# Two experts picked in slot 31 from 14 batches' first choices, and a drain in another order

## The reference

```
logits = x @ gate_w.T
probs = jax.nn.softmax(logits, axis=-1)
top2_w, top2_idx = jax.lax.top_k(probs, 2)
cap = int(CAPACITY_FACTOR * T / E)            # 640 of 4096 tokens
counts = jnp.bincount(top2_idx.reshape(-1), length=E)
keep = (counts <= cap).astype(x.dtype)
comb = jnp.zeros((T, E)).at[jnp.arange(T)[:, None], top2_idx].add(top2_w) * keep[None, :]
h = jax.nn.relu(jnp.einsum('th,ehf->tef', x, W1) + b1)
y = jnp.einsum('teh,ehf->tef', h, W2) + b2
out = jnp.einsum('te,tef->tf', comb, y)
```

## Time and profile before

| | |
|---|---|
| median of three runs | 516.7 us (516.62 to 518.55) |
| profiled execution | 519.01 us, span 517.0 us |
| granted PE clock, mean | 0.993 |
| busy: PE, DVE, ACT, POOL | 499.2, 401.2, 371.2, 324.0 us |

### The profile page before, as it was taken

The page is one execution under the profiler, slowest core; times in us unless marked ns, Lnnn a source line. Parts: engine busy times, 40 slices in busy tenths (PEclk is TensorE's granted clock), DMA queues, the critical chain, the costliest instruction groups (busy, mean ns, idle before and its releaser), DMA issues.

```text
span 517.0 us, 12870 instructions
## 1 busy us (share of the span) xinstructions
PE 499.2 (97%) x3896; PEld 348.6 (67%) x3896; DVE 401.2 (78%) x715; ACT 371.2 (72%) x851; POOL 324.0 (63%) x328
## 2 busy tenths in 40 slices
PE   7899999999999999999999999999999989889997
PEld 6866667666666777766676667666666756666664
DVE  4234788888888888888888888888888797736766
ACT  3467777777777777777777777777777437657873
POOL 1102677777777777777777777777777549004760
PEclk9999999999999999999999999999999989999999
DMA  6500000000000000000000000000000000000004
GB/s 221 155 1 2 2 1 2 1 0 0 0 0 0 0 0 0 0 0 0 0 0 0 0 0 0 0 0 0 0 0 2 1 1 0 2 0 2 0 21 143
DMA packets 9364, 7.19 MB, mean 14 GB/s; under 512 B 1088, under 2 KB 8832, under 8 KB 9216
## 3 DMA queue, kind: packets, MB, share of 16 engines
q1 hardware_dynamic: 9344, 6.94, 4.6%
HBM read 4.84 MB, written 2.10 MB: 13 GB/s over the span
## 4 chain that ended last, share of the span: by engine, by line
PE 89%; DVE 5%; issue 2%; ACT 2%; DMA 1%; SPq 1%; POOL 1%; DVEq 0%; ACTq 0%; POOLq 0%
PE bank_a L704 11%; PE misc L711 11%; PE bank_d L719 11%; PE bank_t L686 11%; PE bank_s L671 7%; PE bank_d L696 6%; PE bank_t L953 4%; PE bank_t L681 4%; PE misc L841 3%; PE misc L843 3%; PE misc L808 2%; PE bank_s L961 2%; PE bank_d L961 2%; PE misc L868 1%; PE bank_a L642 1%
## 5 line engine op out<-in xcount | busy, mean ns | idle before, releaser
L1374 POOL TENSOR_TENSOR pair<-kx 128x1152 f32<-128x1152 f32 x32 | 82.9, 2591 | 96.6 <-DVE shifted L422 77.7
L300 DVE TENSOR_REDUCE row_max<-bank_s 128x4 bf16<-128x512 f32 x128 | 89.4, 699 | 67.7 <-PE bank_s L671 67.7
L1339 POOL TENSOR_TENSOR mix_hi<-mix_hi 128x512 f32<-128x512 f32 (+2 forms) x96 | 79.7, 831 | 3.1
L1007 ACT ACTIVATE qT<-misc 128x512 f32<-128x512 f32 x64 | 39.1, 611 | 53.7 <-PE misc L711 53.6
L1007 ACT ACTIVATE prob<-bank_t 128x512 f32<-128x512 f32 x128 | 69.7, 603 | 4.4 <-PE bank_t L686 2.8
L719 PE MATMUL bank_d<-attT,wpost_sb 128*128 128x128 f32 x512 | 69.2, 278 | 0.2 <-DVE attT L308 0.2
L711 PE MATMUL misc<-yT,wq_sb 128*128 128x128 f32 x512 | 67.7, 275 | 0.0
L704 PE MATMUL bank_a<-prob,v 128*32 128x512 f32 x512 | 67.4, 598 | 0.0
L686 PE MATMUL bank_t<-qT,kT 64*128 64x256 f32 x512 | 65.7, 376 | 0.0
L1345 POOL TENSOR_TENSOR mix_hi<-weight,kx 128x1024 f32<-128x1024 f32 x32 | 63.1, 1973 | 0.3 <-ACT weight L1007 0.3
L711 PEld LDWEIGHTS misc<-yT,wq_sb 128*128 128x128 f32 x512 | 62.2, 192 | 0.8
(11 more groups left out here) (183 smaller groups left out, 934.9 us busy)
## 6 DMA issues: line engine op xcount, KB each, us to landing
out<-acc_all SPq DMA_DIRECT2D x8, 256.0 KB, 2.3
x_all<-in_xT SPq DMA_DIRECT2D x1, 1024.0 KB, 9.7
w_sb<-in_w SPq DMA_DIRECT2D x2, 512.0 KB
x_all<-in_xT SPq DMA_DIRECT2D x1, 768.0 KB, 7.6
wq_sb<-in_wq SPq DMA_DIRECT2D x1, 512.0 KB, 6.2
wpost_sb<-in_wpost SPq DMA_DIRECT2D x1, 512.0 KB, 9.8
x_all<-in_xT SPq DMA_DIRECT2D x1, 256.0 KB, 3.2
b_rows<-in_b SPq DMA_DIRECT2D x16, 4.0 KB
```

The source lines that it names most:

```text
L300: V.tensor_reduce(bass.AP(row_max, first_w * (P + 1) + HPG * p, [[HPG * P, P], [P + 1, 2], [KEY, 2], [1, 1]]), bank_s[:, :, :].rearrange(" ...
L1007: return nc.scalar.activation(out_, in_, func, **kw)
L1339: G.tensor_tensor(mix_hi[:, jd, 0:r, :], mix_hi[:, jd, 0:r, :], mix_hi[:, jd, r:2 * r, :], ALU.add).then_inc(s_hi, 1)
L1374: G.tensor_tensor(pair[:, :, :], bass.AP(kx2, jc * 2 * P, [[4 * P, P], [0, SHIFTS], [1, P]]), bass.AP(kx2, jc * 2 * P, [[4 * P, P], [MD, S ...
```

## The change

1. First choices of 14 batches (COUNTED) instead of 24 make the pick. Logits of batches 0 to 5 and 6 to 13 stay in slot 31, the first group no longer ahead of the last scores; those of 14 to 23 come in the drain, behind unit 0. ACT copies the EARLY logits there, too.
2. `pick_ahead` stands at the end of slot 31, right behind the second `normalise`, instead of in slot 32 behind `weight_sums` and `weight_inverses`. Its intermediate values lie in PSUM (bank_s); the key formula is done twice, once into PSUM and once into SBUF.
3. In slot 32 `weighted_rows` comes before the head copies, `weight_sums` and `weight_inverses` behind the shift. `keys_twice` waits for the first quarter of `s_lo` and `s_hi` (the products that read the keys) only.
4. The count product stands behind units 12 and 13 instead of ahead of them. Only one group of x1 transposes (into misc[1]) comes before the loop's first hidden products, seven behind them; the banks of bank_x are in another order.

```diff
@@ -33,6 +33,7 @@
+COUNTED = range(14)
@@ -157,14 +158,15 @@
-        bank_x = [b[:, :].rearrange("p (t f) -> p t f", f=P) for b in bank_a] + [misc[1][:, :, :]]
+        wide_a = [b[:, :].rearrange("p (t f) -> p t f", f=P) for b in bank_a]
+        bank_x = [misc[1][:, :, :]] + wide_a
         bank_e = [bank_s, bank_d]
-        bank_b = bank_x[0:2] + [misc[0][:, :, :], misc[1][:, :, :]]
+        bank_b = wide_a + [misc[0][:, :, :], misc[1][:, :, :]]
         def key_out(b):
-            return misc[1][:, 0:1, :] if s_is(b, BATCH - 1) else bank_x[1][:, 0:1, :]
+            return misc[1][:, 0:1, :] if s_is(b, BATCH - 1) else wide_a[1][:, 0:1, :]
@@ -354,23 +356,23 @@
-            def ranked(into):
-                step(V.tensor_tensor(t88[:, :, :], key[:, :].unsqueeze(1).to_broadcast(wide),
-                                     key[:, :].unsqueeze(2).to_broadcast(wide), ALU.is_lt))
-                step(V.tensor_reduce(place[:, :], t88[:, :, :], AX.X, ALU.add))
-                step(V.tensor_tensor(t88[:, :, :], index8[:, :].unsqueeze(2).to_broadcast(wide),
-                                     place[:, :].unsqueeze(1).to_broadcast(wide), ALU.is_equal))
-                step(V.tensor_tensor(t88[:, :, :], t88[:, :, :], index8[:, :].unsqueeze(1).to_broadcast(wide), ALU.mult))
-                step(V.tensor_reduce(order_f[:, :], t88[:, :, :], AX.X, ALU.add))
+            def ranked(into, key, same, place, t88):
+                step(V.tensor_tensor(t88, key.unsqueeze(1).to_broadcast(wide),
+                                     same.unsqueeze(2).to_broadcast(wide), ALU.is_lt))
+                step(V.tensor_reduce(place, t88, AX.X, ALU.add))
+                step(V.tensor_tensor(t88, index8[:, :].unsqueeze(2).to_broadcast(wide),
+                                     place.unsqueeze(1).to_broadcast(wide), ALU.is_equal))
+                step(V.tensor_tensor(t88, t88, index8[:, :].unsqueeze(1).to_broadcast(wide), ALU.mult))
+                step(V.tensor_reduce(order_f[:, :], t88, AX.X, ALU.add))
...
-                dve.wait_ge(s_log_mm, 4)
+                dve.wait_ge(s_log_mm, 2)
                 dve.wait_ge(s_const, 3)
-                top, fi = part(r_max, EARLY), part(first, EARLY)
-                lg = misc[0][:, :, :].rearrange("p w f -> p (w f)")[:, 0:len(EARLY) * EXPERTS].rearrange(
+                top, fi = part(r_max, COUNTED), part(first, COUNTED)
+                lg = misc[0][:, :, :].rearrange("p w f -> p (w f)")[:, 0:len(COUNTED) * EXPERTS].rearrange(
@@ -379,10 +381,13 @@
-                step(V.scalar_tensor_tensor(out=key[:, :], in0=bank_s[:, 0, 0:EXPERTS], scalar=float(EXPERTS),
-                                            in1=index8[:, :], op0=ALU.mult, op1=ALU.add))
-                ROUTE_STEPS["pick"] = ranked(ahead_order)
-                step(V.tensor_scalar(not_ahead[:, :], place[:, :], float(AHEAD), None, ALU.is_ge))
+                rank, spot = bank_s[:, 1, 0:EXPERTS], bank_s[:, 1, EXPERTS:2 * EXPERTS]
+                for t in (rank, key[:, :]):
+                    step(V.scalar_tensor_tensor(out=t, in0=bank_s[:, 0, 0:EXPERTS], scalar=float(EXPERTS),
+                                                in1=index8[:, :], op0=ALU.mult, op1=ALU.add))
+                ROUTE_STEPS["pick"] = ranked(ahead_order, rank, key[:, :], spot, bank_s[:, 2, 0:EXPERTS * EXPERTS].rearrange(
+                    "p (a b) -> p a b", b=EXPERTS))
+                step(V.tensor_scalar(not_ahead[:, :], spot, float(AHEAD), None, ALU.is_ge))
@@ -498,23 +503,22 @@
                         normalise(s, 0)
                     if s_is(s, BATCH - 1):
                         normalise(s, 1)
+                        pick_ahead()
                 def drain_slot():
-                    if s == BATCH:
-                        weight_sums()
-                        weight_inverses()
-                        pick_ahead()
                     if C:
                         attended()
                     head_scores()
+                    if s == BATCH:
+                        weighted_rows()
                     own_copies()
                     head_maxima()
                     head_shift()
                     if D:
+                        weight_sums()
+                        weight_inverses()
                         if s > BATCH:
-                            weight_sums()
-                            weight_inverses()
-                        weighted_rows()
+                            weighted_rows()
                         row_sum()
                         rows_joined()
                         mixed()
@@ -721,7 +725,7 @@
-            parts_early = [EARLY[a:b] for a, b in ((0, 6), (6, 13), (13, 19), (19, 24))]
+            parts_early = [EARLY[a:b] for a, b in ((0, 6), (6, 14), (14, 24))]
@@ -730,19 +734,23 @@
+                if tiles == parts_early[2]:
+                    pe.wait_ge(s_rt, ROUTE_STEPS["tops"])
...
-                              tok_all[:, col(b)], gate_sb[:, :], start=(b in (EARLY[0], RECENT[0])), stop=True,
+                              tok_all[:, col(b)], gate_sb[:, :], start=(b in (EARLY[0], parts_early[2][0], RECENT[0])), stop=True,
...
-                pe.wait_ge(s_ao, UNITS)
+                pe.wait_ge(s_kx2, BATCH)
                 for q in quads:
+                    if 0 < q < len(bank_x):
+                        pe.wait_ge(s_ao, UNITS - len(bank_x) + 1 + q)
@@ -810,8 +818,6 @@
-                    if final:
-                        gate_logits(parts_early[0])
@@ -843,7 +849,7 @@
-                        gate_logits(parts_early[1])
+                        gate_logits(parts_early[0])
@@ -859,8 +865,7 @@
-                        gate_logits(parts_early[2])
-                        gate_logits(parts_early[3])
+                        gate_logits(parts_early[1])
@@ -906,7 +911,9 @@
                         ahead_hidden(1)
                         keys_turned(c)
                         pe.wait_ge(s_x1T, n(c))
-                        ahead(0, 1, 2)
+                        ahead(0)
+                        gate_logits(parts_early[2])
+                        ahead(1, 2)
                         mixing_turned(d)
                         ahead(3)
                         tokens_made(d)
@@ -933,11 +940,12 @@
             slots(pe, slot)
+            ahead(12, 13)
             pe.wait_ge(s_log, 2)
             pe.wait_ge(s_rt, ROUTE_STEPS["count"])
             mm(misc[0][:, 0, 0:EXPERTS], ones[:, :], count[:, :], start=True, stop=True).then_inc(s_cnt_mm, 1)
-            ahead(12, 13, 14, 15)
-            x1_transpose(range(HALF))
+            ahead(14, 15)
+            x1_transpose(range(1))
             def bias_rows(quads):
@@ -970,7 +978,7 @@
-            x1_transpose(range(HALF, QUADS))
+            x1_transpose(range(1, QUADS))
@@ -1048,8 +1056,6 @@
-                if tiles[0] in EARLY:
-                    act.wait_ge(s_rt, ROUTE_STEPS["tops"])
@@ -1120,8 +1126,8 @@
-                    need(act, s_lo, 4 * n(c - 2))
-                    need(act, s_hi, 4 * n(c - 2))
+                    need(act, s_lo, 4 * (c - 2) + 1)
+                    need(act, s_hi, 4 * (c - 2) + 1)
@@ -1140,7 +1146,6 @@
-                        copy_logits(EARLY, 4)
@@ -1151,7 +1156,9 @@
                         ahead_relu(1)
                         keys_twice()
                         head_weights()
-                        ahead(0, 1, 2)
+                        ahead(0)
+                        copy_logits(EARLY, 3)
+                        ahead(1, 2)
                         mixing_out(d)
                         ahead(3)
                         tokens_out(d)
@@ -1168,7 +1175,7 @@
-                        copy_logits(RECENT, 6)
+                        copy_logits(RECENT, 5)
@@ -1255,9 +1261,10 @@
             set_expert(0, e)
             runs = act.value_load(n_run[0:1, 0:1], min_val=3, max_val=EXPERTS - 1)
             act.wait_ge(s_b1, 1)
+            copy_x1(range(1))
             for i in range(2):
                 relu(i + 1, i)
-            copy_x1(range(HALF, QUADS))
+            copy_x1(range(1, QUADS))
             act.wait_ge(s_rt, ROUTE_STEPS["loop"])
             set_gate(0, e)
             act.wait_ge(s_gT_mm, 1)
```

More of the change, by code:

```diff
@@ L545, in _ @@
                                         op0=ALU.mult, op1=ALU.add))
-            ROUTE_STEPS["order"] = ranked(order)
+            ROUTE_STEPS["order"] = ranked(order, key[:, :], key[:, :], place[:, :], t88[:, :, :])
             step(V.tensor_reduce(kept[:, :], keep_loop[:, :], AX.X, ALU.add))
@@ L1230, in _ @@
             ahead(12, 13, 14, 15)
-            copy_x1(range(HALF))
             def set_gate(k, e):
```

## The result

In the first comparison (four executions of each kernel in turn on one chip) the changed kernel took 511.6 us in the median (510.87 to 511.86), the kernel before 516.66 us: ratio 0.989, 95% interval 0.987 to 0.992, faster by 5.1 us. The forecast was 510.3 with a range of 508.0 to 513.6.

What follows compares the result with a forecast made beforehand. PE, busy 499.2 of 517.0 us, was the bound. Loop start 8.1 us sooner less 1.64 for extra copies gave 6.4 us (pick 4.0, count 2.4); from the 516.7 us median this made 510.3, range 508.0 to 513.6.

Steps and rivals of the forecast that it cites:

- Slot 31: Logits of ten batches move from slot 31 behind the drain's first unit, so batch 31's normalisation comes 2.27 us sooner.
- The pick: Choosing the first expert on VectorE from PSUM takes 1.8 us instead of 3.2, or 3.4 if GpSimd still slows it.
- First product: PE's first expert product at 417.4 us instead of 421.07, after a stop of 1.1 us, with full clock behind it.
- Unit 1: The drain's unit 1 starts at 423.8 us where it was 426.60, 2.8 us ahead.
- Mixing: Drain: batch 30's mixing follows the pair product 7.7 us later, at 431.5, before PE's 434.8; the 1.22 us stop goes.
- Count: Final count: its 2.24 us stop goes; the loop's first hidden product comes 8.1 us sooner, behind a 2.1 us stop.
- Copies: Loop's first hidden product to gate transposes: seven residual copies instead of four, paced by ScalarE, 6.44 us instead of 4.80.
- Rival 1: Behind the first expert's stop: the clock gain is absent or the low clock stays, 1.4 us less, 511.7 us; chance 0.17.
- 1.42 us regained: First product to first output group: 2.35 us at full clock instead of 3.77 at half clock.
- Rival 2: The remaining 2.1 us stop ahead of the loop lowers the clock, 1.8 us more, 512.1 us; chance 0.08.
- rival 3: Drain: mixing still sets PE's place, the sooner pick buys nothing, only the count's 2.4 us, 514.3 us; chance 0.09.
- Rival 4: Fourteen batches pick an expert the count throws out; the loop runs four experts, 14.9 us more, 525.2 us; chance 0.03.

Runs made afterwards that it cites:

- e4: Changed kernel with the pick's intermediate values back in SBUF and one key formula, at the new place: 512.53 us, ratio 0.991 to the kernel before.
- e7: Changed kernel with the pick's last reduction written to PSUM and the cast reading it there: 510.33 us, ratio 0.986 to the kernel before.
- e8: Changed kernel with the order and waits of the mixing (part 3) as before: 512.53 us, ratio 0.992 to the kernel before.
- e11: e10 with residual copies of groups 2, 4 and 6 moved from ScalarE to VectorE: 510.04 us, ratio 0.985 to the kernel before.
- The parts alone: Kernel before with only parts 1 to 3 (e3, again e12): 514.13 and 514.57 us; with only part 4 (e2): 515.48 us.
- e9: Changed kernel again, no edit: 511.14 us against 518.14 for the kernel before, ratio 0.986.
- e5: Kernel before with 16 dummy products instead of 6 ahead of the pick: 517.79 us, ratio 1.000 to the kernel before.
- e6: Changed kernel without the six dummy products ahead of the pick: 512.50 us, ratio 0.991 to the kernel before.
- e12: Same kernel as e3, run once more: 514.57 us, ratio 0.994 to the kernel before.
- e3: Changed kernel with part 4 undone, so only parts 1 to 3 (pick and mixing): 514.13 us, ratio 0.992 to the kernel before.
- e10: e7 with ScalarE loading the loop's first expert once the order is there, ahead of the number of passes: 509.76 us, ratio 0.985 to the kernel before.
- e2: Kernel before with only part 4 (later count product, one x1 group ahead of the loop): 515.48 us, ratio 0.996 to the kernel before.
- e1: Kernel before again, no edit: 517.39 us, ratio 0.999 to the kernel before.

## Why the prediction was right, step by step

Gains here are before less after, each from its first score product (0.91 us off each difference of starts).

- **Slot 31.** 2.27 us predicted; the second normalisation ended at 412.36 instead of 415.52, 2.25.
- **The pick.** The lower bound of 1.8 us was taken for it; it took 412.28 to 414.88, 2.60. PSUM cost next to nothing (0.23 us a step with 64 values, 0.22 from SBUF in the earlier trace rows), and e4 shows that SBUF would have cost 2.25. The missing term is the cast, the one instruction left with only SBUF operands. I had priced it like its neighbours, at 0.26 with the gap. By the prediction's argument, that an instruction with a single SBUF input is not held up, it was free; the 0.88 us here and the 0.17 of e7 show that for the cast this is false.
- **First product.** 417.4 was predicted, 416.71 measured, of which 0.9 is the shorter start-up: 3.45 us sooner, not 3.67. The stop was 1.34 us (1.1 predicted). The clock stayed at 1.00. From the first product to the first output group it took 2.54 us; 2.35 predicted, 3.77 before.
- **Unit 1.** 2.44 us sooner, not 2.8: about the two misses above, 0.22 and 0.19 us.
- **Mixing.** No stop, as predicted, but with no slack: ready at 434.05 and turned by PE at 434.20, where the forecast had 431.5 (430.6 with the shorter start-up) and 3.3 us of slack. The pair product was on time (419.97). Two terms failed here. The first is "DVE's rest of that slot, about 5 us": batch 29's mix rows, two SBUF operands, took 1.88 us beside POOL's product instead of the 0.29 that the row of before at 426.46 has. By starting POOL sooner part 3 put its product beside them; in e8, without part 3, they took 0.29 again. The second is "follows 7.7 us later": no row gives this number. From DVE's first score step of that slot to the end of batch 30's mix rows it was 9.46 us in the kernel before (429.21 to 438.67) and 9.46 in the changed one (424.59 to 434.05). In the changed one the mix rows took 2.09 us, but they had taken 1.25 before as well, so this part was a misjudged size and no effect of the change. The mixing came 3.5 us later than forecast against 3.3 us of forecast slack, and PE, itself 0.3 us later than forecast, just did not have to stop: that was luck. The 1.22 us of the earlier trace rows came back all the same; e8 shows that without part 3 they would not have. PE began the hidden product of unit 13 (449.57 before, 444.95 now) 3.71 us sooner (4.0 predicted).
- **Count.** No stop there, as predicted; the loop's first hidden product 8.25 us sooner (8.1), behind a stop of 1.54 us (2.1).
- **Copies.** 6.27 us for 6.44. Gates 6.78 us sooner (6.4 predicted). The reason given, that ScalarE paces them, does not hold alone: e11 takes three of the seven copies off ScalarE, and the transposes end no sooner (5.38 us against 5.36).

The sum of 6.4 us stood against 6.6 to 6.9 by the body. The parts alone were predicted at 4.0 and 2.4 and measured at 3.7 and 2.75. That the time came out at 511.6 and not 510.3 is not a failed step. The forecast subtracted it from 516.7, the median of three runs; in later comparisons the kernel before had medians of 517.3 to 518.1 over 11 to 27 executions. That the start-up's scatter made this difference is likely, not shown; it moves the first score product by up to 4 us between profiles. The interval of the first comparison (4.3 to 6.9 us) holds the sum, that of e9 (5.8 to 8.9) too.

**The rivals.** Rival 1 was right on its facts and wrong on its price: the low clock is missing in at least a third of the executions of before (9 of 27), yet e5 shows that losing it gains nothing there, since the mixing covered it. By the same token the forecast's "1.42 us regained" was no gain of the clock alone. It counts only together with part 3, and in the changed kernel the clock matters (e6). Rival 2 (a low stretch ahead of the loop) was in no profile of the changed kernel; rival 3 (mixing still sets the pace) is excluded by e12, and by e8 in size. Rival 4 (four passes) did not happen: the stretch behind the gates is the same in all profiles.

## What to carry to other kernels

When a helper's operands are moved to PSUM to escape GpSimd, move the last small cast too, and price each VectorE step by what GpSimd will do at its new place, not by its duration elsewhere. A clock loss is worth what the next wait doesn't cover: in e5 the 1.1 us regained bought 0.2, in e6's profile its return cost 2.3. And where executions scatter by 4 us in start-up, compare profiles from the first product of the steady work.

## What the runs showed of the hardware

- The granted clock fell to 0.50 with PE busy without a gap, in e3 and e10 at 424 to 428 us behind 20 products with 8 result columns (2.29 us); in e2 it averaged 0.58 over 411 to 415 us, behind 22 such products of slot 31 (408.39 to 411.01). It did not behind the 20 in e12 and the changed kernel's two profiles, nor behind the 22 in the profiles of before, e1 and e5. In e3 against e12 it cost 1.33 us. The Trainium skill (TensorE: Matmul & The Clock Gate, HAM oscillation) names idle gaps as what lowers the clock; these rows show a fall without one.
- In the stretch of the two experts, stops of 2.51 to 2.63 us (profiles of before, e1, e4, e6) were each followed by 0.50; those of 2.24, 1.54 and 1.34 us were not. The length alone does not decide: in start-up, stops of 1.94 us (e2) and 2.15 us (e9) were followed by 0.50, 1.1 to 1.3 us behind their end, and in four of e4's seven executions the mean clock was 1.000.
- A cast of 8 values from SBUF took 0.88 us beside POOL's sums and 0.17 with POOL idle; a reduction of 64 values from SBUF took 0.22 beside the same sums (e4).
- Start-up differs by two levels that the granted clock does not tell: the second row of dummy products took 3.35 us for 14 in seven profiles (the changed kernel among them) and 1.83 in the seven others, with the windows at 1.00 in both. What sets this stays open. Of the seven quick ones six then stood 1.94 to 3.23 us for the transfer of wq_sb and had 0.50 behind it; e6 stood 1.46 us, kept 1.00 and has the soonest first score product.
